# A quad of edges in four transfers, each one run of memory, in a fused graph-network step

## The chip, the cores and the metric

The kernel runs on one core of a Trainium2 chip. The metric is the time on the device in microseconds (us), the median of the runs. A profile of one execution gives the span from the first instruction to the last.

## The reference

12500 nodes with 128 features, 200000 edges with 128 features, sorted by the node they point to. The edges of a node are summed, the normalised nodes and the sums go through three layers, and the normalised result is added to x. All is float32.

```python
agg = jax.ops.segment_sum(edge_attr, col, num_segments=x.shape[0])   # col = dst
h = jnp.maximum(_layernorm(x), 0.0)
h = jnp.concatenate([h, agg], axis=-1)
h = jax.nn.relu(h @ W1 + b1)
h = jax.nn.relu(h @ W2 + b2)
h = h @ W3 + b3
out = x + layernorm(h) * ln_w + ln_b
```

The edges are 102 MB; x and the output are 6.4 MB each.

## The kernel before

**Edges.** A chunk is 384 consecutive edges: partition p of 128 holds edges 3p to 3p + 2, a run of 1536 bytes. A quad is four chunks, 1536 edges, 768 KB. There are 130 quads and a last chunk. SP loads quads into `ring`, eight slots of 6144 bytes a partition; each slot has a semaphore `edges_loaded`. For one quad the source is seen as `p s (j f)`: each partition takes four runs of 1536 bytes, one of each chunk, and they lie 192 KB apart in memory. One DMA instruction moves the whole quad.

**Sums.** For a quad PE waits for its slot (`seg`, L402), then does 12 products of one-hot matrices with edges, 24 instructions in the trace, since each float32 product is two passes (L410). Each chunk adds into a window of 32 nodes, a quarter of the rows of one `part_ps`. ACT copies these partial sums to `part` (L619). `put` multiplies them by a placement matrix that POOL makes (L761), which moves them to 128 consecutive nodes (L421), and DVE adds them to `agg` (L911). DVE makes the one-hot matrices for two quads at a time (L893).

**Layers.** A group is 384 nodes. While quads go on, PE does the three layers of one group for every four quads (L438, L445, L455, L461). DVE and ACT normalise. One such step of four quads and one group is the body of every engine's loop; the loops hold two steps, with the two parities of the buffers written out.

**The order on SP.** All loads and nearly all stores are issued by SP, so they go through one queue. At the start: dst (L269 to L274), quad 0 (L283), the rest group and groups 0 and 1 of x, quads 1 to 7 (L289), group 2 of x (`load_x`, L281). Then the branch on a flag that DVE computes from dst (L257). In the fast branch `reload(q, slot)` waits on `seg_done` until PE is through with the quad that held the slot, eight quads earlier, and issues the next (L308, L309). Ten quads and one group of x are written out singly. Then a loop runs 4 times and a second one 10 times, and each turn has two steps: a group of x and four quads, twice. The first loop also stores two groups a turn (`store_two`, L304). After the loops come the last chunk (L331), eleven stores of two groups, and the rest. In the loops the address of a transfer is computed in registers ahead of it.

**The counts.** Each transfer adds 16 to its slot's semaphore when it has landed. So quad q of a slot is there when the semaphore has reached 16 x (q // 8 + 1). PE waits so at L402 and L536, and the branch that is not taken in these runs has such waits on SP and DVE.

Of the kernel before, what the change touches and what calls it, by code (L numbers as in the profile page):

```python
# [30 lines left out]
P = 128  # L31
# [3 lines left out]
PER = 3  # L35
CHUNK = P * PER
WIN = 32
QC = P // WIN
QUAD = QC * CHUNK
QUADS = EDGES // QUAD  # L40
CHUNKS = QUADS * QC
TAIL0 = EDGES - CHUNK
DONE = CHUNKS * CHUNK - TAIL0
OCT = 2 * QC
GROUPS = NODES // CHUNK
LAST = GROUPS
LAST0 = GROUPS * CHUNK
LAST_PER = 2
# [7 lines left out]
RING = 8  # L56
# [13 lines left out]
STORED_EARLY = 8  # L70
STEPS = GROUPS - 1


def gnn_kernel(nc, x, dst, edges, w1, b1, w2, b2, w3, b3, lnw, lnb, out):
    assert GROUPS == 32 and QUADS == 4 * STEPS + AHEAD and LAST_P * LAST_PER == LAST_N and RC * RP == REST
    with ExitStack() as ctx:
# [3 lines left out]
        def sem(name):  # L80
            return ctx.enter_context(nc.semaphore(name))
# [7 lines left out]
        local_t = sb("local_t", [P, PER, NCOL])  # L89
        onehot = sb("onehot", [P, 2, OCT, PER, WIN])  # L90
        part = sb("part", [P, 2, D])
# [81 lines left out]
        edges_loaded = [sem(f"edges_loaded{k}") for k in range(RING)]  # L173
# [47 lines left out]
        full_out_ready = sem("full_out_ready")  # L221
        stored = sem("stored")

        def quad_of_edges(q):

            return edges[bass.ds(q * QUAD, QUAD), :].rearrange("(s p j) f -> p s (j f)", p=P, j=PER)

        def ring_slot(k):
            return ring[:, k, :].rearrange("p (s e) -> p s e", s=QC)
# [33 lines left out]
        with nc.Block() as block:  # L263
# [3 lines left out]
            def _(sp):  # L267
# [12 lines left out]
                        sp.wait_ge(x_loaded[par], 16 * before)  # L280
                    sp.dma_start(xg(g), group_rows(x, g)).then_inc(x_loaded[par], 16)  # L281

                sp.dma_start(ring_slot(0), quad_of_edges(0)).then_inc(edges_loaded[0], 16)  # L283
                for p0, p1 in LAST_PARTS:
                    sp.dma_start(xg(LAST)[p0:p1, :], last_rows(x, p0, p1)).then_inc(last_x_loaded, 16)
                load_x(0, 0, 0)
                load_x(1, 1, 0)
                for q in range(1, RING):
                    sp.dma_start(ring_slot(q), quad_of_edges(q)).then_inc(edges_loaded[q], 16)  # L289
                for g in range(2, XAHEAD):  # L290
                    load_x(g, g % 2, g // 2)

# [13 lines left out]

                def reload(q, slot):
                    sp.wait_ge(seg_done, q - RING + 1)  # L308
                    sp.dma_start(ring_slot(slot), quad_of_edges(q)).then_inc(edges_loaded[slot], 16)  # L309

                def fast():
                    for q in range(RING, RING + AHEAD):
# [26 lines left out]
                def general():  # L339

                    d2 = dst_i[:, :, :].rearrange("p t k -> p (t k)")
                    sp.dma_start(d2[:, 0:BLOCKS * BLOCK].rearrange("p (b c) -> p b c", c=BLOCK),
                                 dst[0:BLOCKS * P * BLOCK].rearrange("(b p c) -> p b c", p=P, c=BLOCK)
                                 ).then_inc(dst2_loaded, 16)
                    sp.dma_start(d2[0:RP, BLOCKS * BLOCK:BLOCKS * BLOCK + RC],
                                 dst[EDGES - REST:EDGES].rearrange("(p c) -> p c", c=RC)).then_inc(dst2_loaded, 16)
                    for k in range(RING):
                        sp.wait_ge(edges_loaded[k], 16)
                    sp.dma_start(ring[0:RP, 4, 0:RC * D],
                                 edges[EDGES - REST:EDGES, :].rearrange("(p c) f -> p (c f)", c=RC)).then_inc(rest_loaded, 16)  # L350
                    with sp.Fori(0, WINDOWS) as w:
                        with sp.Fori(0, BLOCKS // 2) as b:
                            for par in range(2):

                                sp.wait_ge(block_done, w * BLOCKS + 2 * b + par + 1)
                                sp.dma_start(ring[:, par, :],
                                             edges[bass.ds((2 * b + par) * P * BLOCK, P * BLOCK), :]
                                             .rearrange("(p c) f -> p (c f)", c=BLOCK)).then_inc(block_loaded[par], 16)
                    load_x(XAHEAD, XAHEAD % 2, XAHEAD // 2)
                    with sp.Fori(2, GROUPS // 2) as t:  # L360
                        load_x(2 * t, 0, t)
                        load_x(2 * t + 1, 1, t)
                    with sp.Fori(0, GROUPS) as g:
                        store(g)
                    store_last(GROUPS + 1)
                    sp.wait_ge(stored, 16 * (GROUPS + len(LAST_PARTS)))
# [5 lines left out]
            def _(pe):  # L372
# [26 lines left out]
                def seg(q, par_q, load_count, oct_ready=None):  # L399

                    slot = par_q % RING
                    pe.wait_ge(edges_loaded[slot], load_count)  # L402
                    if oct_ready is not None:
                        pe.wait_ge(onehot_ready, oct_ready)
                    e = ring_slot(slot)
                    oct_par, first = (par_q // 2) % 2, (par_q % 2) * QC

                    for j in range(PER):
                        for s in range(QC):
                            last = nc.tensor.matmul(part_ps[par_q % 2][s * WIN:(s + 1) * WIN, 0:D],  # L410
                                                    onehot[:, oct_par, first + s, j, :],
                                                    e[:, s, j * D:(j + 1) * D], start=(j == 0), stop=(j == PER - 1))
                    last.then_inc(seg_done, 1)
# [65 lines left out]
                def fast():  # L479
                    pe.wait_ge(wts_loaded, 9 * 16)  # L480
                    for q in range(AHEAD):
                        seg(q, q, 16, q // 2 + 1)
                        if q >= 1:
                            put(q - 1, q - 1, free=q >= 3)
                    transpose_h(0)

                    def step(i, par, pairs):


                        for k in range(4):  # L490
                            turn_q = 4 * par + AHEAD + k
                            q = 4 * i + AHEAD + k
                            seg(q, turn_q, 16 * (pairs + turn_q // RING + 1),
                                2 * i + AHEAD // 2 + k // 2 + 1 if k % 2 == 0 else None)
                            put(q - 1, turn_q - 1)
                            if k == 0:
                                layer1(i, 4 * i + AHEAD - 1)
                            elif k == 1:
                                layer2(i)
                            elif k == 2:  # L500
                                layer3(i)
                            else:
                                transpose_h(i + 1)

                    step(0, 0, 0)
                    with pe.Fori(0, (STEPS - 3) // 2) as t:
                        step(2 * t + 1, 1, t)
                        step(2 * t + 2, 0, t + 1)
                    step(STEPS - 2, 1, (STEPS - 2) // 2)

                    q, g = QUADS - 4, GROUPS - 2

                    def loads_of(quad):
                        return 16 * (quad // RING + 1)

                    layer1_x(g)
                    seg(q, q, loads_of(q), q // 2 + 1)
                    put(q - 1, q - 1)  # L520
                    layer1_sums(g, q - 1)
                    put(q, q)
                    transpose_h(g + 1)
                    seg(q + 1, q + 1, loads_of(q + 1))
                    layer2(g)
                    put(q + 1, q + 1)
                    layer1_x(g + 1)
                    seg(q + 2, q + 2, loads_of(q + 2), q // 2 + 2)
                    layer3(g)
                    put(q + 2, q + 2)  # L530
                    seg(q + 3, q + 3, loads_of(q + 3))
                    layer1_sums(g + 1, QUADS - 1)
                    put(q + 3, q + 3)
                    slot = QUADS % RING
                    pe.wait_ge(onehot_ready, QUADS // 2 + 1)
                    pe.wait_ge(edges_loaded[slot], loads_of(QUADS))  # L536
                    for j in range(PER):
                        last = nc.tensor.matmul(part_ps[QUADS % 2][0:WIN, 0:D], onehot[:, (QUADS // 2) % 2, 0, j, :],
                                                ring[:, slot, j * D:(j + 1) * D], start=(j == 0), stop=(j == PER - 1))
                    last.then_inc(seg_done, 1)  # L540
                    layer2(g + 1)
                    layer1_x(LAST)
                    put(QUADS, QUADS, rows=WIN)
                    layer3_last_bias()
                    layer3(g + 1)
                    layer1_sums(LAST, QUADS + 1)
                    layer2(LAST)
                    layer3_last()
# [258 lines left out]
            def _(dve):  # L807
# [265 lines left out]
                def general():  # L1073
# [3 lines left out]
                    dve.wait_ge(agg_zeroed, 1)  # L1077
                    dve.wait_ge(wts_loaded, 9 * 16)
                    for k in range(RING):
                        dve.wait_ge(edges_loaded[k], 16)  # L1080
                    nc.vector.memset(place[:, 0, :], 0.0).then_inc(zeros_ready, 1)
                    nc.vector.memset(local[RP:P, BLOCKS * BLOCK:BLOCKS * BLOCK + RC], -1.0)
                    dve.wait_ge(dst2_loaded, 32)
# [61 lines left out]
```

## Time and profile before

| | |
|---|---|
| timed runs | 323.63, 326.09, 327.76 us; median 326.09 |
| span of the profiled execution | 323.9 us (its own time on the device isn't given beside it) |
| PE busy | 273.6 us (84%) |
| DVE busy | 255.8 us (79%) |
| POOL busy | 179.8 us (56%) |
| ACT busy | 148.9 us (46%) |
| moved by DMA | 116.68 MB, 360 GB/s over the span |
| chain that ended last | SP's queue 43%, PE 25%, DMA 16%, DVE 8% |

Instructions that issue a DMA are not counted as busy; in the chain they stand as "SPq". Of PE the matrix products are counted, not its weight loads, which run beside them (PEld). The time of a DMA from issue to landing is counted from the start of its issue instruction.

### The profile page before, as it was taken

Reading aid. Unit: us, or ns where it says so; the run is one execution under the profiler, and the core shown is the slowest. Engines: PE = TensorE matmul, PEld = TensorE weight load, DVE = VectorE, ACT = ScalarE, POOL = GpSimd, SP = SyncE. Lnnn points to the kernel's source line nnn. Section 1 sums busy time; section 2 is a strip of 40 time slices with the busy share of each in tenths; the row PEclk is TensorE's granted clock in tenths of the full one; section 3 lists DMA queues with packets and bytes.
Section 4 is the critical chain, followed back from the end, with each engine's and each line's share of the span. In section 5 each row is a group of like instructions: output and inputs, shape, how many; then the busy total and the mean of one; then the engine's idle time right before and its main releaser. Section 6 shows DMA issues by size and latency. Waiting matters only on the chain.

```text
span 323.9 us, 12307 instructions
## 1 busy us (share of the span) xinstructions
PE 273.6 (84%) x3925; PEld 186.8 (58%) x3925; DVE 255.8 (79%) x944; ACT 148.9 (46%) x406; POOL 179.8 (56%) x208
## 2 busy tenths in 40 slices
PE   0176999899998898799888898888888889988991
PEld 0045766666666565566565566555656656655660
DVE  8975458888989777588878787787787877877985
ACT  1052255555555544255455544444555555444632
POOL 9506355556666545566655555556566555555541
PEclk9995799999999999799999999999999999999997
DMA  7996999999999999999999999999999999999995
GB/s 234 323 373 218 299 372 373 371 378 378 373 384 373 385 373 382 376 373 373 372 373 373 373 373 373 373 373 373 373 373 373 373 373 373 373 373 374 373 397 213
DMA packets 79880, 116.68 MB, mean 360 GB/s; under 512 B 3357, under 2 KB 79866, under 8 KB 79866
## 3 DMA queue, kind: packets, MB, share of 16 engines
q1 hardware_dynamic: 78426, 115.85, 101.6%
q10 hardware_dynamic: 1440, 0.66, 0.9%
q8 instruction: 7, 0.11, 0.1%
q14 instruction: 7, 0.06, 0.1%
HBM read 110.09 MB, written 6.40 MB: 360 GB/s over the span
## 4 chain that ended last, share of the span: by engine, by line
SPq 43%; PE 25%; DMA 16%; DVE 8%; issue 6%; ACT 1%; DVEq 0%; ACTq 0%
SPq L309 30%; DMA ring<-in_edge_attr 16%; PE part_ps L410 9%; SPq L281 9%; PE place_ps L421 4%; DVE widx L845 3%; PE hid_ps L438 2%; SPq L304 2%; PE hid_ps L445 2%; PE hid_ps L455 2%; PE y_ps L461 2%; DVE onehot L893 1%; SPq L308 1%; PE part_ps L378 1%; DVE least L848 1%
## 5 line engine op out<-in xcount | busy, mean ns | idle before, releaser
L761 POOL TENSOR_SCALAR place<-iota,rows_at 128x128 f32<-128x128 f32 x131 | 105.0, 805 | 104.9 <-PE place_ps L421 96.4
L410 PE MATMUL part_ps<-ring,onehot 128*32 128x128 f32 x3120 | 115.8, 283 | 24.2 <-DMA ring<-in_edge_attr 22.0
L410 PEld LDWEIGHTS part_ps<-ring,onehot 128*32 128x32 f32 x3120 | 80.1, 112 | 69.8 <-issue 50.0
L911 DVE TENSOR_TENSOR agg<-place_ps,agg 128x128 f32 x131 | 37.9, 289 | 52.8 <-PE place_ps L421 52.2
L769 POOL TENSOR_TENSOR xs<-xs,lnbs 128x384 f32 (+2 forms) x33 | 54.9, 1664 | 27.0 <-ACT h L633 27.0
L421 PE MATMUL place_ps<-place,part 128*128 128x128 f32 (+1 forms) x262 | 64.8, 330 | 1.3 <-ACT part L619 1.3
L893 DVE TENSOR_TENSOR onehot<-iota,local_t 128x768 f32<-128x768 f32 x66 | 62.8, 953 | 1.2 <-DVE flag_i L887 0.8
L421 PEld LDWEIGHTS place_ps<-place,part 128*128 128x128 f32 (+1 forms) x262 | 40.0, 192 | 28.3 <-issue 19.8
L619 ACT ACTIVATE part<-part_ps 128x128 f32<-128x128 f32 x131 | 34.8, 267 | 46.1 <-PE part_ps L410 45.2
L633 ACT ACTIVATE h<-xs,x_shift,x_rstd 128x128 f32 (+2 forms) x98 | 41.3, 483 | 3.2 <-DVE x_shift L832 3.2
L649 ACT ACTIVATE hid<-hid_ps,b1s 128x384 f32<-128x384 f32 (+1 forms) x33 | 19.0, 576 | 46.2 <-PE hid_ps L445 46.2
L970 DVE SCALAR_TENSOR_TENSOR xs<-z,y_rstd,xs 128x128 f32 (+1 forms) x93 | 32.5, 401 | 4.1
L461 PE MATMUL y_ps<-w3s,hid 128*128 128x128 f32 x192 | 29.7, 291 | 0.0
L625 ACT ACTIVATE x_std<-x_mv,eps 128x3 f32<-128x3 f32 (+1 forms) x33 | 9.8, 297 | 42.0 <-DVE x_mv L820 42.0
L952 DVE SCALAR_TENSOR_TENSOR z<-y,y_mv,lnws 128x128 f32<-128x128 f32 x96 | 28.9, 354 | 0.1
L642 ACT ACTIVATE h_t<-ht_ps 128x384 f32<-128x384 f32 x32 | 22.4, 699 | 13.6 <-PE ht_ps L430 13.6
L438 PE MATMUL hid_ps<-h_t,w1x 128*128 128x384 f32 x64 | 26.7, 500 | 0.8 <-ACT h_t L642 0.8
L455 PE MATMUL hid_ps<-hid,w2s 128*128 128x384 f32 (+1 forms) x66 | 26.8, 487 | 0.5 <-ACT hid L649 0.5
L445 PE MATMUL hid_ps<-agg,w1a 128*128 (+2 forms) x66 | 26.6, 484 | 0.0
L461 PEld LDWEIGHTS y_ps<-w3s,hid 128*128 128x128 f32 x192 | 23.8, 191 | 1.4 <-issue 0.5
L812 DVE BATCH_NORM_STATS2 x_stats<-xs 128x6 f32 (+2 forms) x98 | 21.9, 278 | 0.0
L936 DVE BATCH_NORM_STATS2 y_stats<-y 128x6 f32<-128x128 f32 x96 | 20.8, 272 | 0.1
(83 smaller groups left out, 221.6 us busy)
## 6 DMA issues: line engine op xcount, KB each, us to landing
ring<-in_edge_attr SPq DMA_DIRECT2D x130, 768.0 KB, 11.6
xs<-in_x SPq DMA_DIRECT2D x32, 192.0 KB, 10.0
out_x<-xs SPq DMA_DIRECT2D x15, 384.0 KB
dst_i<-in_dst SPq DMA_DIRECT2D x1, 768.0 KB
ring<-in_edge_attr SPq DMA_DIRECT2D x1, 192.0 KB, 10.5
out_x<-xs SPq DMA_DIRECT2D x1, 192.0 KB
out_x<-xs ACTq DMA_DIRECT2D x1, 192.0 KB
xs<-in_x SPq DMA_DIRECT2D x1, 96.0 KB
```

The lines of the kernel that those rows point to most:

```text
L309: sp.dma_start(ring_slot(slot), quad_of_edges(q)).then_inc(edges_loaded[slot], 16)
L410: last = nc.tensor.matmul(part_ps[par_q % 2][s * WIN:(s + 1) * WIN, 0:D], onehot[:, oct_par, first + s, j, :], e[:, s, j * D:(j + 1) * D], ...
L421: nc.tensor.matmul(place_ps[par_q % 2][:, 0:P], part[0:rows, par_q % 2, :], place[0:rows, par_q % 2, :], start=True, stop=True).then_inc(p ...
L438: nc.tensor.matmul(hid1_ps[:, 0:n], w1x[:, :], t[:, :], start=True, stop=False)
L455: nc.tensor.matmul(hid2_ps[:, 0:n], w2s[:, :], hid1[:, 0:n], start=True, stop=True).then_inc(hid2_done, 1)
L461: last = nc.tensor.matmul(y_ps[:, j * D:(j + 1) * D], hid2[:, j, :], w3s[:, :], start=True, stop=True)
L619: nc.scalar.activation(part[0:rows, par_q % 2, :], part_ps[par_q % 2][0:rows, 0:D], ACT.Copy).then_inc(part_copied, 1)
L633: last = nc.scalar.activation(h[0:rows, j, :], xg(g, j), ACT.Relu, bias=x_shift[0:rows, j:j + 1], scale=x_rstd[0:rows, j:j + 1])
L761: nc.gpsimd.tensor_scalar(place[:, par_q % 2, :], iota[:, 0:P], rows_at[:, k:k + 1], None, ALU.is_equal).then_inc(place_ready, 1)
L769: nc.gpsimd.tensor_tensor(v, v, lnbs[0:rows, :].unsqueeze(1).to_broadcast([rows, per, D]), ALU.add).then_inc(x_biased, 1)
L893: nc.vector.tensor_tensor(onehot[:, par % 2, :, :, :], iota[:, 0:WIN].unsqueeze(1).unsqueeze(1).to_broadcast([P, OCT, PER, WIN]), local_t[ ...
L911: nc.vector.tensor_tensor(v, place_ps[par_q % 2][:, 0:P], v, ALU.add).then_inc(added, 1)
```

## The change

`quad_of_edges(q)` with its four-fold source goes, and `chunk_of_edges(q, s)` takes its place: the 384 edges of one chunk, which are one run of 192 KB in memory. A new `load_quad` issues four transfers in a row, chunk s into the s-th quarter of the slot, each adding 16 to the slot's semaphore. So a slot's count grows by 64 for a quad (`LANDED`), and every wait is written with it. The last chunk is still one transfer and adds 16.

```diff
+LANDED = 16 * QC
...
-        def quad_of_edges(q):
-
-            return edges[bass.ds(q * QUAD, QUAD), :].rearrange("(s p j) f -> p s (j f)", p=P, j=PER)
+        def chunk_of_edges(q, s):
+
+            return edges[bass.ds(q * QUAD + s * CHUNK, CHUNK), :].rearrange("(p j) f -> p (j f)", j=PER)
...
-                sp.dma_start(ring_slot(0), quad_of_edges(0)).then_inc(edges_loaded[0], 16)
+                def load_quad(q, slot):
+                    for s in range(QC):
+                        sp.dma_start(ring_slot(slot)[:, s, :], chunk_of_edges(q, s)).then_inc(edges_loaded[slot], 16)
+
+                load_quad(0, 0)
...
-                    sp.dma_start(ring_slot(q), quad_of_edges(q)).then_inc(edges_loaded[q], 16)
+                    load_quad(q, q)
...
                 def reload(q, slot):
                     sp.wait_ge(seg_done, q - RING + 1)
-                    sp.dma_start(ring_slot(slot), quad_of_edges(q)).then_inc(edges_loaded[slot], 16)
+                    load_quad(q, slot)
...
-                        seg(q, q, 16, q // 2 + 1)
+                        seg(q, q, LANDED, q // 2 + 1)
...
-                            seg(q, turn_q, 16 * (pairs + turn_q // RING + 1),
+                            seg(q, turn_q, LANDED * (pairs + turn_q // RING + 1),
...
-                        return 16 * (quad // RING + 1)
+                        return LANDED * (quad // RING + 1)
...
-                    pe.wait_ge(edges_loaded[slot], loads_of(QUADS))
+                    pe.wait_ge(edges_loaded[slot], LANDED * (QUADS // RING) + 16)
```

The instructions change on SP alone. In SP's loop, before, from the transfer of x in the middle of the body (ISA and REGISTER_ALU are register work; ISA carries the wait):

```order
L281 ISA [waits x_loaded_odd]
L281 DMA xs<-in_x 128x384
L308 ISA
L309 ISA [waits seg_done]
L309 DMA ring<-in_edge_attr 128x4x384
L308 REGISTER_ALU
L309 ISA [waits seg_done]
L309 DMA ring<-in_edge_attr 128x4x384
```

The same place after, where L282 is `load_x`, L286 `load_quad` and L313 `reload`:

```order
L282 ISA [waits x_loaded_odd]
L282 DMA xs<-in_x 128x384
L313 ISA
L286 ISA [waits seg_done]
L286 DMA ring<-in_edge_attr 128x384
L286 ISA
L286 DMA ring<-in_edge_attr 128x384
L286 ISA
L286 DMA ring<-in_edge_attr 128x384
L286 ISA
L286 DMA ring<-in_edge_attr 128x384
L313 REGISTER_ALU
```

One DMA instruction over 128 x 4 x 384 elements has become four over 128 x 384, with one register instruction ahead of each of the three added ones, and no further wait.

## Rows read from the trace of the kernel before

**Rows 1.** The page, parts 2 and 3: GB/s in 40 slices; the first queue.

```profile
GB/s 234 323 373 218 299 372 373 371 378 378 373 384 373 385 373 382 376 373 373 372 373 373 373 373 373 373 373 373 373 373 373 373 373 373 373 373 374 373 397 213
...
q1 hardware_dynamic: 78426, 115.85, 101.6%
```

**Rows 2.** Busy time in one stretch: length, PE, PEld, DVE, ACT, POOL, clock, DMA share, GB/s.

```profile
202.40:220.30 17.90, 15.89 (x239) 10.83 (x239) 14.34 (x57) 8.71 (x24) 10.43 (x13) 1.00 1.06 373
```

**Rows 3.** The view of line L410: what ended its idle time (us, times).

```profile
  DMA ring<-in_edge_attr: 34.6, 43
```

**Rows 4.** SP's waits between 20 and 66 us: total us, times, longest.

```profile
SPq L309 <- PE part_ps L410: 25.6, 17, 3.1
```

**Rows 5.** The chain that ended last, pieces of SP and one of PE: start, us, what.

```profile
81.87 1.80 SPq L304
...
84.54 0.36 SPq L281
...
207.35 0.05 issue
207.40 0.03 SPq L308
207.43 0.03 issue
207.46 0.06 SPq L309
207.52 0.04 issue
207.56 0.03 SPq L309
207.59 0.03 issue
207.62 1.78 SPq L309
...
210.05 1.39 SPq L281
...
211.76 0.37 SPq L309
...
217.92 0.05 issue
...
218.15 2.39 SPq L281
...
310.05 0.79 PE part_ps L410 x24
```

**Rows 6.** Views of L309 and L281: ns min/median/max, first and last start; landing.

```profile
L309 SPq DMA_DIRECT2D ring<-in_edge_attr x122: 367/1559/2499, 27.8 to 297.1; - x122
...
DMA to landing us min/median/max: 4.6/11.6/12.3
...
L281 SPq DMA_DIRECT2D xs<-in_x x32: 355/1420/2387, 3.4 to 289.8; - x32
```

**Rows 7.** Views of L604 and L274, two of nine and one: ns min/median/max.

```profile
L604 ACTq DMA_DIRECT2D w3s<-in_L_gnn_W x1: 453/453/453, 2.2 to 2.2; - x1
...
L604 ACTq DMA_DIRECT2D lnbs<-in_L_gnn_ln_b x1: 882/882/882, 4.7 to 4.7; - x1
...
L274 SPq DMA_DIRECT2D dst_i<-in_dst x1: 235/235/235, 1.7 to 1.7; - x1
```

**Rows 8.** DMA issues: count, KB each, us to landing.

```profile
w1x<-in_L_gnn_W ACTq DMA_DIRECT2D x1, 64.0 KB, 3.0
```

**Rows 9.** SP's own order of time: start, us taken together, line, count.

```profile
4.38 14.62 SPq L289 DMA_DIRECT2D ring<-in_edge_attr  x7
...
39.73 6.68 SPq L309 DMA_DIRECT2D ring<-in_edge_attr  x4
...
303.91 4.28 SPq L304 DMA_DIRECT2D out_x<-xs  x4
```

More of the change, by code:

```diff
@@ L347, in general @@
                     for k in range(RING):
-                        sp.wait_ge(edges_loaded[k], 16)
+                        sp.wait_ge(edges_loaded[k], LANDED)
                     sp.dma_start(ring[0:RP, 4, 0:RC * D],
@@ L1079, in general @@
                     for k in range(RING):
-                        dve.wait_ge(edges_loaded[k], 16)
+                        dve.wait_ge(edges_loaded[k], LANDED)
                     nc.vector.memset(place[:, 0, :], 0.0).then_inc(zeros_ready, 1)
```

## The prediction

> **What bounds the kernel now.** I read the page's lines on the DMA first: 373 GB/s for slice after slice, and the first queue's packets take 101.6% of the engines' span [rows 1]. The table of stretches confirms it for one double step (a turn of SP's loop: 8 quads and 2 transfers of x) in the middle: in 17.90 us PE, the busiest engine, has 15.89 us of work, and the DMA share is 1.06 at 373 GB/s [rows 2]. So the DMA engines are the bound there. The reader should then look at who waits. PE's L410 waits for `ring`, 34.6 us in 43 places, PE and its weight loads together [rows 3]. SP waits for PE too, 25.6 us in 17 places, all of them between 20 and 66 us: while eight quads are still loaded ahead, PE sets the pace there [rows 4].
>
> The chain shows how SP stands in the steady part. An issue instruction of a quad takes 1.78 us there, with 0.27 us of register work and gaps ahead of it; the one right behind a transfer of x takes 0.37 us [rows 5]. The long ones are a full queue pushing back: a quad issued there lands 11.6 us later by the median and at best 4.6 us later [rows 6], so some 9 to 10 us of traffic stand ahead of it. Unhindered the instruction takes 367 ns for a quad and 355 ns for 128 rows of x [rows 6]. So SP has slack that the profile doesn't name as such: of each 17.9 us (8 quads, 2 transfers of x) it needs only 10 x 0.37 us plus the gaps, and waits out the rest inside its issue instructions. The change spends this slack.
>
> **The change, part by part.** (a) Each quad becomes four issue instructions with a register instruction before each; only the first waits for `seg_done`. In the loop a double step issues 34 transfers in place of 10. (b) The bytes are the same, and each transfer is still made of runs of 1536 bytes, 128 of them instead of 512. (c) The counts on the eight semaphores go from 16 to 64 a quad, and the waits of PE, DVE and SP with them. PE waits for the whole quad as before; this costs nothing in itself, since the number of instructions on PE and DVE is unchanged.
>
> The price of (a), from rows. Issue instruction: 0.368 us each, the value of L309 without a queue; x's minimum of 0.355 us shows that a quarter of the rows makes it hardly cheaper [rows 6]. Ahead of the first transfer of a quad the gap stays 0.27 us (one register instruction at L308, one fused at L309, one move), or 0.32 us right behind x. Ahead of each of the other three there is a fused instruction and a move: without L308's 0.03 us and the 0.04 us beside it that leaves 0.20 us [rows 5]. Ahead of x the gap is 0.23 us in the middle of the loop body and 0.65 us across its end [rows 5]. One double step on SP is then
>
> 34 x 0.368 = 12.51; 24 x 0.20 = 4.80; 6 x 0.27 + 2 x 0.32 = 2.26; 0.23 + 0.65 = 0.88; sum 20.45 us.
>
> The DMA engines need 17.9 us for the same bytes. So SP, which had slack, becomes the bound by some 2.5 us a double step, about 14%. The queue runs nearly empty, and each transfer lands soon after its issue.
>
> The first part of the kernel hides its share. At the start 28 issues stand where 7 did; the nine transfers that ACT issues back to back take 0.45 us each by the median and 0.88 us at most [rows 7], 0.49 us with the 0.04 us of a gap, and so the 28 take 13.7 us, where the 7 took 14.6 us against a full queue. SP ends that part well before the branch, behind which L309 starts only at 27.8 us [rows 6, 9]. From there the ten quads written out singly, and one x, cost (40 + 1) x 0.49 = 20.1 us, up to 47.9 us; before, they were paced by PE and done at 46.4 us [rows 9], so 1.5 us are lost here. Then come 14 double steps: 14 x 20.45 = 286.3 us. Four of them also store two groups: an issue of 0.37 us with 0.23 us ahead of it, as for x, and 0.22 us more at the loop's end than without a store (0.87 us from the store's issue to that of x, against 0.65) [rows 5], together 3.3 us. SP is done at 47.9 + 286.3 + 3.3 = 337.5 us, where it was at about 299 us (297.1 us for the last start [rows 6] and a long issue). The last quarter of quad 129 is issued at 337.1 us. It lands 3.0 us later: that is what 64 KB take unhindered, and also the 4.6 us of an unhindered quad less three quarters of its 2.1 us of traffic [rows 6, 8]. PE starts on quad 129 at 340.1 us. Before, PE started on it at 310.05 us, and from there the kernel had 13.9 us to go, nearly all of it PE and DVE work in a chain [rows 5]; this stays. The stores held back for the end take 1.07 us each when the queue is full [rows 9]: 11 of them from 338 us on are through by about 350 us, so they don't end last. Span: 340.1 + 13.9 = 354.0 us. The profile gives the span of 323.9 us and no time of its own execution beside it; the median of the timed runs is 2.2 us above the span, which I add: **356.2 us**, 9% slower.
>
> Two prices are not in the trace, and I bound them. What an issue costs 0.20 us behind another one: at least the 0.235 us of SP's transfer of a single row of dst, at most ACT's 0.453 us [rows 7]; the nearest rows are the 0.355 and 0.367 us of rows 6. I take 0.368, since behind x, with a gap of 0.32 us, it is still 0.37 us [rows 5]; at 0.45 us the loop would take 14 x 34 x 0.08 = 39 us more. What a separate transfer costs on the DMA engines: each adds 16 small packets for its count. At nothing they are free; taken as dear as a packet of data (17.9 us over 272 data packets and 10 others on an engine, 0.064 us), they bring the engines to 17.9 + 24 x 0.064 = 19.4 us a double step, still under SP's 20.45. That the DMA engines are faster over one run of memory than over four interleaved ones is possible too, and under SP's bound it would gain nothing.
>
> The Trainium skill (DMA: Bandwidth & Descriptors, "Issuing engines are not separate DMA queues") says that the sequencer's time to start a DMA is usually small relative to the DMA itself. Here the row of 0.37 us stands against 0.53 us of traffic for 192 KB, so the trace doesn't bear this out for this size. The same page ("Anatomy of one DMA") puts dispatch at about 50 ns and generation at small; by that the sum would be the first rival's.
>
> **Rivals.**
> A, the other side: issues overlap. The 0.37 us might be mostly latency that shrinks when the transfer is smaller or follows closely. SP decides nothing as long as 34 issues with their gaps fit into 17.9 us, 0.527 us apiece, that is an issue of at most 0.29 us beside 0.23 us of gaps. Then the DMA engines stay the bound. For it: the transfer of one row of dst took 0.235 us [rows 7]. Against it: 128 and 512 rows cost the same to 12 ns [rows 6]. It would give 326 us, with the small packets free; if one run of memory were also served faster, PE would be next with its 15.89 us of work a double step [rows 2], 14 x 2.0 = 28 us less at most, some 298 us. I see nothing in the profile that speaks for that.
> B, dearer issues: 0.45 us each. Time 356 + 39 = 395 us; for it, ACT's nine; against it, ACT's had a gap of 0.04 us only, and its interval of 0.49 us is shorter than the 0.57 us here, so the longer gap may pay for it.
> C, separate transfers are dear on the engines. Long issues of quads in the chain end 2.05 us apart (209.40 and 211.44 us); eight such in a stretch of 17.90 us would leave 0.75 us for each x, where its bytes alone need 0.53 [rows 2, 5]. A quad of four such would take 3.0 us, a double step 34 x 0.75 = 25.5 us, and the kernel 324 + 14 x 7.6 = 430 us or a little more. Against it: stores of 384 KB follow each other in 1.07 us, just half a quad's 2.1 us [rows 9].
>
> **How the numbers follow.** Forecast, SP's issues as the bound at about 0.34 to 0.40 us each (342 to 372 us): 0.70. A: 0.11, of which 0.03 for the faster memory. B and what lies between it and the forecast (372 to 400 us): 0.14. C: 0.05. The range reaches from 342 us (14 us less, 0.03 us off each of the loop's 476 issues) to 386 us (0.06 us on each), most of the way to B. About 2% is what a measurement of this kernel can tell from no change. Faster by over 2%: 0.03; within 2%: 0.08; slower: 0.89.
>
> **What would show it.** In the profile after: no issue instruction in the loop near 1.78 us, all near 0.37 to 0.40 us; SP's double step near 20.5 us and the DMA rate at 373 x 17.9 / 20.45 = 327 GB/s; the landing of a quarter about 3 us after its issue in place of 10 to 12; PE's waits for `ring` up by about 2.5 us a double step; SP's waits for PE shorter in the stretch up to 66 us. The forecast is wrong if SP still shows long issues (then the queue is still full, A or C, told apart by the GB/s), or if they sit at 0.45 us or more without a full queue (B).

## The result and the profile after

| | before | after |
|---|---|---|
| median of the timed runs | 326.20 us | 344.58 us (343.43 to 345.08) |
| ratio | | 1.056, 95% interval 1.051 to 1.062 |
| span of the profiled execution | 323.9 us | 341.7 us (343.43 us on the device) |
| DMA rate in the loop | 373 GB/s | 350 GB/s |

The forecast was 356.2 us in a range of 342 to 386. The change makes the kernel slower, by 18.4 us and not by 30.

The page after, the GB/s of its 40 slices and its first queue:

```profile
GB/s 223 353 366 231 331 358 329 339 362 350 363 353 365 350 345 349 360 350 359 349 339 356 331 366 338 362 341 355 355 341 363 330 356 353 354 343 344 325 386 242
...
q1 hardware_dynamic: 84666, 115.87, 98.7%
```

Against [rows 1] the even run of 373 is gone: no slice of the loop reaches it. The packets have grown by 6240, 16 for each of the 390 added transfers. Now one double step of SP's loop, from one transfer of x to the one two steps on, in the columns of [rows 2]:

```profile
188.34:207.45 19.11, 17.14 (x234) 11.32 (x237) 14.07 (x56) 8.62 (x24) 9.61 (x12) 0.91 1.03 348
```

19.11 us stand where 17.9 stood. The DMA share of 1.03 looks as full as before; by this row alone one could hold the engines for the bound. SP's order of time says otherwise (start, us taken together, line, count):

```profile
188.34 0.35 SPq L282 DMA_DIRECT2D xs<-in_x  x1
189.01 8.45 SPq L286 DMA_DIRECT2D ring<-in_edge_attr  x16
197.69 0.35 SPq L282 DMA_DIRECT2D xs<-in_x  x1
198.35 8.44 SPq L286 DMA_DIRECT2D ring<-in_edge_attr  x16
207.45 0.35 SPq L282 DMA_DIRECT2D xs<-in_x  x1
```

Sixteen issues take 8.45 us with their gaps, again and again, and x 0.35 us: nothing is held up by a full queue. The chain shows the pieces, where [rows 5] had an issue of 1.78 us:

```profile
200.53 0.33 SPq L286
200.86 0.05 issue
200.91 0.05 SPq L286
200.96 0.04 issue
200.99 0.03 SPq L286
201.02 0.03 issue
201.05 0.33 SPq L286
```

An issue of 0.33 us and a gap of 0.19 to 0.20 us: 0.525 us for 192 KB. The view of L286, to set against [rows 6], with the landing and the waits of PE:

```profile
L286 SPq DMA_DIRECT2D ring<-in_edge_attr x520: 328/333/1517, 2.0 to 322.1; - x174
...
  PE part_ps L415: 33.9, 27
  PEld part_ps L415: 15.2, 28
...
DMA to landing us min/median/max: 2.4/3.7/7.1
```

The median issue is the unhindered one, a quarter lands after 3.7 us where a quad took 11.6, and PE with its weight loads waits 49.1 us for `ring` against 34.6 [rows 3]. SP's own wait for PE [rows 4] is down from 25.6 to 3.9 us:

```profile
SPq L286 <- PE part_ps L415: 3.9, 4, 2.9
```

### The profile page after: what moved, and what is told of

It reads as the page before. It is cut to its first block, busy times and chain, and to the rows that moved or that the text cites. A ratio compares the mean times of both kernels' runs of the same rounds, so it can differ in the third digit from the quotient of the medians.

```text
span 341.7 us, 13369 instructions
## 1 busy us (share of the span) xinstructions
PE 278.5 (82%) x3925; PEld 188.1 (55%) x3925; DVE 258.6 (76%) x944; ACT 148.7 (44%) x406; POOL 175.4 (51%) x208
## 4 chain that ended last, share of the span: by engine, by line
SPq 40%; PE 25%; issue 14%; DMA 12%; DVE 7%; ACT 1%; DVEq 0%; ACTq 0%
SPq L286 36%; DMA ring<-in_edge_attr 12%; PE part_ps L415 10%; PE place_ps L426 4%; DVE widx L850 3%; SPq L282 3%; PE hid_ps L443 2%; PE hid_ps L450 2%; PE y_ps L466 2%; PE hid_ps L460 1%; SPq L313 1%; PE part_ps L383 1%; DVE least L853 1%; DVE onehot L898 1%; PE ht_ps L435 0%
## 5 line engine op out<-in xcount | busy, mean ns | idle before, releaser
L766 POOL TENSOR_SCALAR place<-iota,rows_at 128x128 f32<-128x128 f32 x131 | 102.5, 784 | 128.3 <-PE place_ps L426 119.5
L898 DVE TENSOR_TENSOR onehot<-iota,local_t 128x768 f32<-128x768 f32 x66 | 64.7, 982 | 1.3 <-DVE flag_i L892 0.8
L774 POOL TENSOR_TENSOR xs<-xs,lnbs 128x384 f32 (+2 forms) x33 | 51.8, 1571 | 25.5 <-ACT h L638 25.5
L975 DVE SCALAR_TENSOR_TENSOR xs<-z,y_rstd,xs 128x128 f32 (+1 forms) x93 | 31.4, 390 | 4.1
L957 DVE SCALAR_TENSOR_TENSOR z<-y,y_mv,lnws 128x128 f32<-128x128 f32 x96 | 30.4, 371 | 0.1
L443 PE MATMUL hid_ps<-h_t,w1x 128*128 128x384 f32 x64 | 29.2, 541 | 0.8 <-ACT h_t L647 0.8
L450 PE MATMUL hid_ps<-agg,w1a 128*128 (+2 forms) x66 | 28.3, 512 | 0.0
```

The source lines that it names most:

```text
L443: nc.tensor.matmul(hid1_ps[:, 0:n], w1x[:, :], t[:, :], start=True, stop=False)
L450: nc.tensor.matmul(hid1_ps[:, 0:n], w1a[:, :], agg[:, bass.ds(g * CHUNK, n)], start=False, stop=True).then_inc(hid1_done, 1)
L766: nc.gpsimd.tensor_scalar(place[:, par_q % 2, :], iota[:, 0:P], rows_at[:, k:k + 1], None, ALU.is_equal).then_inc(place_ready, 1)
L774: nc.gpsimd.tensor_tensor(v, v, lnbs[0:rows, :].unsqueeze(1).to_broadcast([rows, per, D]), ALU.add).then_inc(x_biased, 1)
L898: nc.vector.tensor_tensor(onehot[:, par % 2, :, :, :], iota[:, 0:WIN].unsqueeze(1).unsqueeze(1).to_broadcast([P, OCT, PER, WIN]), local_t[ ...
```

## The experiments

Two theories were set against each other. SP: issuing 34 transfers takes SP longer than the engines need for their bytes. ENGINES: each separate transfer costs the DMA engines time, and SP only looks busy. All ratios are to runs of the kernel before on the same chip; the changed kernel itself was not run again beside the experiments.

**Two transfers a quad.** The changed kernel, but

```diff
-LANDED = 16 * QC
+LANDED = 16 * 2
...
-                    for s in range(QC):
+                    for s0, s1 in ((0, 2), (2, 4)):
```

each with two chunks in it.

> A quad in two transfers of two chunks each: SP issues 18 transfers a double step, which by the profile after costs it about 8 x (0.63 + 0.53) + 1.6 = 11 us, far below the 17.9 us of the DMA engines. Theory SP (the changed kernel is slow because issuing 34 transfers takes SP 19.1 us a double step): the time goes back to that of the kernel before, 326 to 328 us. Theory ENGINES (each separate transfer costs the DMA engines time, (19.1 - 17.9) / 24 = 0.05 us): one third of the 18.4 us remains, about 332 us, and the DMA rate in the loop is about 365 GB/s.

Measured: 325.67 us, ratio 1.001 (0.998 to 1.005). The stretch in the middle of its loop:

```profile
150.00:220.00 70.00, 62.25 (x931) 42.44 (x935) 55.87 (x220) 33.88 (x93) 40.50 (x48) 1.00 1.06 373
```

373 GB/s, as before. ENGINES wanted 365 and 332 us.

**Three transfers a quad**: two chunks, one, one.

> A quad in three transfers (two chunks, one, one): 26 transfers a double step, about 8 x (0.63 + 2 x 0.53) + 1.6 = 15 us on SP. Theory SP: still hidden behind 17.9 us of the DMA engines, so 326 to 329 us, and the step from three to four is the whole loss. Theory ENGINES: two thirds of the loss, about 338 us.

Measured: 326.63 us, ratio 1.004 (1.001 to 1.007), and again 373 GB/s in the loop:

```profile
150.00:220.00 70.00, 62.59 (x931) 42.64 (x928) 56.25 (x221) 33.93 (x93) 41.22 (x48) 1.00 1.06 373
```

The loss does not grow with the count of transfers; nearly all of it comes with the fourth, the step at which SP's sum passes the 17.9 us of the engines. Its chain still shows issues of 0.84 us beside those of 0.33, so the queue pushes back and SP has slack:

```profile
201.86 0.84 SPq L286
...
202.93 0.33 SPq L286
```

**Four transfers, SP's loops written out.** The changed kernel with both loops as Python loops:

```diff
-                    with sp.Fori(0, STORED_EARLY // 2) as t:
+                    for t in range(STORED_EARLY // 2):
...
-                    with sp.Fori(STORED_EARLY // 2, (STEPS - 3) // 2) as t:
+                    for t in range(STORED_EARLY // 2, (STEPS - 3) // 2):
```

> The changed kernel (four transfers of one run each) with SP's loops written out, so that no register instruction stands between two issues: 0.04 us of gap in place of 0.20. Theory SP: an issue of 0.33 us and the gap of 0.04 make 34 x 0.37 = 12.6 us, SP is no bound, the long issues of a full queue come back, and the time is 326 to 329 us. Theory ENGINES: nothing changes, 344 us. Should the issue itself grow by what the gap loses (0.49 us, as ACT's at the start), then SP stays at 34 x 0.53 = 18 us and the time is between, about 330 us.

Measured: 329.06 us, ratio 1.015 (1.009 to 1.020). A double step, in the columns of rows 2:

```profile
203.48:221.29 17.81, 15.80 (x239) 10.78 (x238) 14.25 (x57) 8.71 (x24) 10.34 (x13) 1.00 1.07 373
```

The same 34 transfers of the same runs of memory now pass at 373 GB/s. That is the clearest verdict on ENGINES: a separate transfer costs the engines nothing that can be seen here, and one run of memory is read no faster here than four interleaved ones. The view of its L286 adds a fact:

```profile
L286 SPq DMA_DIRECT2D ring<-in_edge_attr x33: 429/432/852, 199.7 to 217.6; - x33
```

Without the register work the issue takes 0.43 us in place of 0.33: it gives back 0.10 of the 0.16 us that the gap loses. The interval is 0.47 us, and 34 of them are 16.1 us, less than the 17.8 us of the engines; the issues of 0.85 us are the queue pushing back again. About 1.5% remain against the kernel before, 3.3 us of the span, and their cause is open. The double step itself is not longer. The timelines of DVE show where the time goes: two of its last three one-hot matrices come 1.3 us later than in the kernel before (301.75 and 305.40 us against 300.45 and 304.10), but the last one 3.5 us later (311.24 against 307.70), and it stands in the chain, where PE stood before. Between them DVE stands idle for 1.4 us with no releaser in the profile. So some 2 us are lost in the last 20 us of the kernel; why is not shown.

**The kernel before, loops written out**, the same edit as a control.

> Control for the run before this one: the kernel before (one transfer a quad) with the same loops written out. Both theories: 326 us, within 1% of the kernel before, since SP waits out its time in the issues.

Measured: 325.10 us, ratio 1.000 (0.997 to 1.003). Writing the loops out is worth nothing where SP has slack.

**A dose on SP.** The changed kernel with one small instruction more ahead of three of the four transfers:

```diff
+                        if s:
+                            sp.sem_inc(sp_went_on, 1)
```

> The changed kernel with one more small instruction on SP (an increment of an unused semaphore) ahead of the second, third and fourth transfer of each quad; DMA traffic unchanged. Theory SP (34 issues and their gaps fill SP's 19.1 us a double step): each added instruction lengthens the double step by itself and its gap, 0.06 to 0.10 us, 24 of them 1.4 to 2.4 us, so 14 double steps 20 to 34 us: 365 to 379 us. Theory ENGINES (the DMA engines set the 19.1 us, their share being 1.02): nothing changes, 344 us. In the part before the loop the issue may give back what the gap takes.

Measured: 367.74 us, ratio 1.131 (1.125 to 1.136), that is 23.2 us above the changed kernel's 344.58 us (24.1 us by the two ratios, since each ran beside its own runs of the kernel before). Its double step and its order of time:

```profile
179.42:200.22 20.80, 17.57 (x240) 11.60 (x238) 14.87 (x57) 8.72 (x24) 9.18 (x13) 0.92 0.98 322
```

```profile
180.10 9.30 SPq L289 DMA_DIRECT2D ring<-in_edge_attr  x16
189.63 0.35 SPq L283 DMA_DIRECT2D xs<-in_x  x1
190.29 9.14 SPq L289 DMA_DIRECT2D ring<-in_edge_attr  x16
```

20.80 - 19.11 = 1.69 us, 0.070 us for each of 24 instructions, 17 ns of it the instruction itself and the rest gaps. 14 x 1.69 = 23.7 us, which is what the whole kernel lost, 23 to 24 us. SP's time in the loop goes into the end one to one.

**The part ahead of the loop.** The changed kernel, but the 18 quads that are written out ahead of the loop come as one transfer each; SP adds the missing 48 to the slot's count itself.

```diff
+                def load_whole(q, slot):
+                    src = edges[bass.ds(q * QUAD, QUAD), :].rearrange("(s p j) f -> p s (j f)", p=P, j=PER)
+                    sp.dma_start(ring_slot(slot), src).then_inc(edges_loaded[slot], 16)
+                    sp.sem_inc(edges_loaded[slot], LANDED - 16)
...
+                    if isinstance(q, int):
+                        load_whole(q, slot)
+                        return
```

> The changed kernel, but the 18 quads written out ahead of SP's loop come as one transfer each, as before (the slot's count is filled up to 64 by SP itself); in the loop four transfers a quad. Theory SP: the first loop issue comes at about 46.9 us as in the kernel before, and not at 50.2 us, so the whole is 3.3 us shorter, 341 us; the rest of the loss, some 15 us, stays, being the loop's. If the part ahead of the loop carried more of the loss, the time is nearer to 335 us.

Measured: 344.96 us, ratio 1.062 (1.057 to 1.067): no gain over the changed kernel. The expectation missed. The loop did start earlier:

```profile
46.38 1.47 SPq L282 DMA_DIRECT2D xs<-in_x  x1
...
69.24 0.36 SPq L282 DMA_DIRECT2D xs<-in_x  x1
...
187.87 0.35 SPq L282 DMA_DIRECT2D xs<-in_x  x1
```

The first transfer of x in the loop is at 46.38 us, in the changed kernel at 50.23. But after the first turn of the loop 1.9 us of this lead of 3.9 us are left (69.24 against 71.09), and by 188 us only 0.5 us (187.87 against 188.34). The first part is not lost to waits for PE: SP waits for PE for 13.9 us here against 3.9, but all of it before 46.3 us, ahead of the loop. What the first turn shows are longer issues: x takes 1.47 us and two of the edges 1.0 us each, where the changed kernel has a single one of 1.30 us. The rest went because the same loop body takes 19.40 us a turn here (168.47 to 187.87 us) in place of 19.11; where in memory the instructions lie differs, but why this costs 0.3 us is open. So this run doesn't isolate the part ahead of the loop. It shows that this part carries little of the loss: the lead that outlived the first turn was 1.9 us, of 18.4.

**Cut by partitions.** Four transfers a quad, each 32 partitions with their four runs:

```diff
+            return edges[bass.ds(q * QUAD, QUAD), :].rearrange("(s p j) f -> p s (j f)", p=P, j=PER)[a * WIN:(a + 1) * WIN, :, :]
...
-                        sp.dma_start(ring_slot(slot)[:, s, :], chunk_of_edges(q, s)).then_inc(edges_loaded[slot], 16)
+                        sp.dma_start(ring_slot(slot)[a * WIN:(a + 1) * WIN, :, :], part_of_edges(q, a)).then_inc(edges_loaded[slot], 16)
```

> Four transfers a quad as in the changed kernel, but cut by partitions: 32 partitions, each with its four runs of 1536 bytes that lie 192 KB apart, in place of 128 partitions and one run of memory. Same count of transfers, bytes and packets. Theory SHAPE (an issue costs 0.367 us where the transfer has a third dimension, as the quads of before, and 0.333 us where it has two, as the quarters): the double step grows by 32 x 0.035 = 1.1 us, about 360 us. Theory ROWS (fewer rows make it cheaper): 344 us or less. Memory order: if interleaved runs are slower to read, the landing in the loop rises and the time goes beyond 360 us; if order doesn't matter, it doesn't.

Measured: four runs of 418, 429, 509 and 510 us, too far apart for a median to mean much; the fastest is 29% above the kernel before (324.50 us). The profile is of a run of 509 us, with a mean granted clock of 0.82 where the run of 418 us had 0.91, so its rate is not that of the fastest run. One double step and the landing:

```profile
200.72:230.61 29.89, 19.63 (x238) 12.79 (x238) 14.75 (x53) 8.02 (x23) 7.55 (x12) 0.83 1.10 222
```

```profile
L286 SPq DMA_DIRECT2D ring<-in_edge_attr x520: 312/566/2952, 2.0 to 480.0; - x174
...
DMA to landing us min/median/max: 5.4/12.4/14.9
```

SP's issues are long again (0.566 us by the median, against 0.312 at best) and a quarter lands after 12.4 us, so here the queue is full and the DMA engines are the bound, at 222 GB/s with the same bytes and packets. Over the whole span this run moved 230 GB/s; the fastest one moved the same 116.7 MB in a span of 416.0 us, an estimate of 281 GB/s. An issue of three dimensions is at its best 0.312 us here, cheaper than the quarter's 0.328, so the number of dimensions alone doesn't set its price as SHAPE had it.

**The same cut with long runs**: 32 partitions with one run of 6144 bytes each. It asks whether the cut or the interleaved memory was to blame.

```diff
-            return edges[bass.ds(q * QUAD, QUAD), :].rearrange("(s p j) f -> p s (j f)", p=P, j=PER)[a * WIN:(a + 1) * WIN, :, :]
+            return edges[bass.ds(q * QUAD, QUAD), :].rearrange("(p s j) f -> p s (j f)", p=P, j=PER)[a * WIN:(a + 1) * WIN, :, :]
```

> Four transfers a quad, each 32 partitions with one run of 6144 bytes each, so that each transfer is one run of 192 KB of memory; the sums are of other edges. Told apart is why the cut by partitions with runs of 1536 bytes fell to 228 GB/s. Theory PARTITIONS (32 neighbouring partitions in one transfer are badly spread over the engines or their ports): the rate stays far below 373 GB/s, the time above 400 us. Theory MEMORY (32 x 4 runs of 1536 bytes 192 KB apart are slow to read): the rate is back at 350 GB/s or more and SP's issues are the bound again, 330 to 350 us.

Measured: 412.37 us from two runs, ratio 1.267 (1.247 to 1.287). Two stretches of it:

```profile
100.00:200.00 100.00, 74.75 (x934) 49.07 (x928) 56.83 (x222) 34.41 (x94) 33.93 (x46) 0.85 1.03 282
200.00:300.00 100.00, 75.45 (x1104) 50.63 (x1102) 72.33 (x260) 40.43 (x113) 38.25 (x58) 0.98 1.03 314
```

One run of 192 KB in memory, and still 282 to 314 GB/s, against 415 for the same length of runs over 128 partitions (below). So the cut by partitions is at fault, and not the interleaved memory. Longer runs bring nothing that can be told here: the whole span has 286 GB/s, as the estimate of 281 for the fastest run of the cut before. The rate also moves within the run, from 233 to 266 GB/s in the slices between 20 and 150 us to 293 to 347 behind them, until the last two slices. How the partitions are spread over the engines the profile doesn't show; why the rate moves is open too.

**Longer runs.** The kernel before, one transfer a quad, with partition p taking 12 consecutive edges as one run of 6144 bytes, by the same edit in `quad_of_edges`.

> The kernel before, still one transfer a quad, but partition p takes edges 12p to 12p + 11 of the quad, one run of 6144 bytes, in place of four runs of 1536. This changes which edges stand in which chunk, so the sums are of other edges; instructions and bytes are the same. It asks whether the 373 GB/s are a matter of the runs' length. If they are: the loop's double step falls from 17.9 us towards PE's 15.9 us of work, 326 - 14 x (1 to 2) = 298 to 312 us. If they aren't (bytes alone, or order in memory without effect): 326 us.

Measured: 301.84 us, ratio 0.932 (0.927 to 0.936). And **runs of 3072 bytes**, with `j=2 * PER` and the slot seen as two halves:

> The kernel before, one transfer a quad, but a partition takes two runs of 3072 bytes (six consecutive edges each) in place of four of 1536; the sums are of other edges. With 6144 bytes the loop ran at 415 GB/s and PE had become the bound. Theory RUN LENGTH (each packet costs the engines something beside its bytes): by bytes / (rate) of 1536 at 373 GB/s the fixed part is at least 65.9 - 59.2 = 6.7 ns a packet of 1536 bytes on an engine, so 3072 bytes run at 393 GB/s or more, the double step is 17.0 us or less, and the time 326 - 14 x 0.9 = 313 us or less, down to the 302 us of 6144. If length had a step (only runs as long as a whole row of the slot are fast): 326 us.

Measured: 311.46 us, ratio 0.959 (0.949 to 0.968). A stretch of each, 6144 bytes first:

```profile
100.00:200.00 100.00, 100.00 (x1503) 68.32 (x1506) 89.42 (x354) 54.74 (x149) 66.95 (x77) 1.00 1.02 415
```

```profile
100.00:200.00 100.00, 95.60 (x1435) 65.42 (x1432) 85.25 (x337) 52.83 (x145) 63.05 (x73) 1.00 1.03 401
```

The stretch of 3072 bytes is close to PE's bound too: PE is busy for 95.6 of 100 us there. With 6144 bytes PE is busy without a break and SP waits for it, which the waits of SP confirm:

```profile
SPq L309 <- PE part_ps L410: 138.5, 105, 2.9
```

Neither is a version of the kernel, since other edges stand in the chunks. They show what the kernel's 373 GB/s are made of: runs of 1536 bytes.

## Why the prediction was right, and where its size was off

*SP becomes the bound.* Right, and shown from both sides: less work on SP between the same transfers (329 us) and fewer transfers (326 us) take the loss away (but for 1.5% in the first case), and more work on SP adds to it at the computed rate. The double step is a sum of SP's instructions, and the long issues are gone.

*34 issues at 0.368 us.* This term was mis-sized. The quarter's issue takes 0.333 us and x's 0.352, so the 34 make 32 x 0.333 + 2 x 0.352 = 11.4 us, not 12.51. I had taken the price of a quad's issue, with x's 0.355 us as a sign that form hardly matters; the range of 0.34 to 0.40 us for the likeliest case just missed it. It is the form that counts, and not the bytes: with runs of 6144 bytes a whole quad is a transfer of two dimensions over 128 partitions, like a quarter, and its issue takes 0.333 us by the median (L309 of that kernel, 327/333/343 ns); half a quad in the kernel with two transfers still has three dimensions and takes 0.367 us at best. The gaps were nearly right, 19.11 - 11.4 = 7.7 us against 7.94. The double step came to 19.11 in place of 20.45 us, and 14 x 1.34 = 18.8 us is more than the whole miss of 12.3 us in the span. With this error alone the forecast would have been 356.2 - 18.8 = 337.4 us, below its own range of 342 to 386; the other misses, most of them the other way, put the time back inside it. So the mechanism was forecast, but that the time lies in the range is in part luck.

*The part ahead of the loop* was mis-sized the other way. The ten quads and x were issued by 49.7 us, not 47.9, though they began at 27.2 us and not at 27.8. The issues stood 0.47 us apart, about as assumed (0.49), but three of them took 1.3 to 1.5 us, and SP waited for PE for another 1.0 us. At the start of the kernel the 28 issues took 15.3 us in place of 13.7, which stayed hidden as forecast.

*The loop's other terms.* The four double steps with a store take 20.86, 19.83, 19.86 and 20.19 us, together 4.3 us more than four without. 1.0 us of it is a single long issue of edges (1.30 us) in the first; the rest is the forecast 3.3 us.

*The end.* The last quarter's issue was put at 337.1 us and came at 322.1: +1.8 us from the part ahead of the loop, -18.8 from the double steps, +1.0 from the long issue, +0.8 from an issue of x of 1.19 us in the last double step, and 0.2 us of rounding and small gaps. PE began on quad 129 5.6 us after it, not 3.0:

```profile
319.89 5.79 DMA ring<-in_edge_attr
325.68 0.04 issue
325.72 0.86 PE part_ps L415 x24
...
327.69 0.86 PE part_ps L415 x24
```

The pieces of PE at 325.72 and 327.69 us are quads 128 and 129. The last quarter of quad 128 took 5.79 us to land; that of quad 129, issued at 322.07, took 5.6, so it landed at 327.6, just as PE came to it. In the loop up to 310 us no quarter took more than 5.0, and the median was 3.7. The last chunk and the stores are issued right behind these two; that they are the reason is not shown. From 327.69 us to the end are 14.0 us, as the 13.9 us carried over from [rows 5]. Sum of the misses: 322.1 - 337.1 + 5.6 - 3.0 + 0.1 = -12.3 us, the span's 341.7 against 354.0. The 2.2 us added for the time on the device were 1.7 in the profiled run, and the median of the runs lies 1.2 us above that run.

*What hides what.* DMA at 327 GB/s was forecast and is 350. SP's waits for PE went, as said. PE's waits for `ring` grew by 14.5 us, but not where they were forecast, 2.5 us in each double step. In the second loop they hardly grew: 30.8 us in ten double steps before (121.5 to 299 us), 29.6 us in nine after (131 to 303 us), 3.1 and 3.3 us a double step. The growth lies in the first loop (3.8 to 10.3 us) and in the last double step and behind it (from 303 us on 9.2 us, where the kernel before has none from 299 us on). That sign of the forecast failed: the step grew by only 1.2 us, and the waits for `ring` are only a part of the time in which PE does nothing.

*The clock.* In the stretch shown PE has 17.14 us of work where it had 15.89, at a granted clock of 0.91, a mean of time at 2.4 and at 1.2 GHz, where it was 1.00 in the kernel before. In the next double step (207.45 to 226.56 us) the clock is 1.00 and PE has 16.04 us of work, and the step is 19.11 us long as well. So the clock doesn't set the double step; SP does.

*The rivals.* A is refuted: issues do not overlap, their 0.33 us stand one behind the other, though they got cheaper than a quad's. Its point of decision, 0.527 us an issue with its gap, was the right one to compute; for 26 transfers the same point is 17.9 / 26 = 0.688 us, and that kernel stays on the good side of it. The quarters reach 0.525 us among themselves; it is the additional gaps ahead of each quad and around x that lift the mean to 19.11 / 34 = 0.562. B is refuted in the loop and true where nothing lies between two issues, 0.43 us. C is refuted: 18, 26 and 34 transfers all pass at 373 GB/s. The small packets, bounded between nothing and 0.064 us, can't be told from nothing: with all of them the double step of the loops written out is 17.81 us, against 17.90 before.

*What the Trainium skill states.* The dispatch of about 50 ns (DMA: Bandwidth & Descriptors, "Anatomy of one DMA — SWDGE (gpsimd) path") belongs to transfers that GpSimd issues. Here SP issues them, so the forecast should not have drawn a sum from it; the row for SP is 0.333 us. The same page's advice to coalesce many small transfers into one large one ("Rules for kernel authors") agrees with these runs in part: one transfer a quad (326.2 us) is faster than four (344.6 us), by way of the issuing engine and not of the DMA engines, but no faster than two or three.

## What to carry to other kernels

Where transfers are issued by one engine, write down its sum as for any other engine: issues x 0.33 to 0.37 us plus the register work between them, per unit of work, against what the DMA engines need for its bytes. Until that sum passed the engines' time, splitting cost nothing here, and from then on every further instruction on the queue's engine went into the end one to one; the limit lay between 26 and 34 transfers for 6.7 MB. In these runs transfers over all 128 partitions with longer runs were the fastest. An issue instruction of well over its minimum, 1.78 us against 0.37, was waiting for a full queue; before it is taken for work, compare it with the minimum in its row and look at the landing times. The gap ahead of it counts as well: 0.43 us was an unhindered issue where only 0.04 us stood before it.

## What was not expected of the hardware

- The price of an issue follows what stands before it: 0.33 us with 0.19 us of register work ahead, 0.43 us with a gap of 0.04 us. Quarters issued one right behind the other stand 0.47 us apart; only the first after a pause on SP is followed after 0.37 us (27.21 and 27.58 us).
- The length of runs still counts above 1536 bytes: 373, 401 and, with PE as the bound, 415 GB/s for 1536, 3072 and 6144 bytes. Estimate from the first two: an engine takes 65.9 ns for a packet of 1536 bytes (16 x 1536 / 373), and 122 ns for one of 3072 (a double step of 6.68 MB at 401 GB/s, 16.7 us, less 16 packets of x, over 128 packets), so some 9 to 10 ns of each packet don't depend on its length. PE was nearly the bound in the second, so this may be a little too small.
- Transfers over 32 partitions are slower at the same count and bytes: 418 us in the fastest run with runs of 1536 bytes and 412 us with 6144, at 281 (estimate) and 286 GB/s over the span, and down to 222 GB/s in a run of 509 us.
- A DMA share above 1 does not prove that the engines are the bound: it is 1.03 at 348 GB/s, with SP as the bound, and 1.07 at 373.
